# Two variances as mean squares on ScalarE, three query-key remainders on GpSimd, and new instruction orders in a one-core transformer layer

## The reference

```python
x = x + layernorm(attention(layernorm(x)))       # 16 heads of 64, T = 256
x = x + layernorm(ffn(layernorm(x)))
# attention: Q, K, V = x W + b; softmax(Q K^T / 8) V, then W_O and b_O
# ffn: gate = softmax(x @ gate_w.T) over 8 experts
#      out  = x @ weight.T + (1/16) * sum_e gate_e * lora_V[e] @ (lora_U[e] @ x)
# layernorm: (x - mean) / sqrt(var + 1e-5), no scale, no shift
```

## Time and profile before

| | us |
|---|---|
| median of three runs (1117.55 to 1120.37) | 1117.65 |
| the profiled execution, whole | 1118.4 |
| its span, first to last instruction | 1116.6 |
| busy in the span: PE | 1018.4 |
| DVE | 1022.7 |
| ACT | 833.8 |
| POOL | 678.0 |

### The profile page before, as it was taken

One profiled execution on the slowest core, in us unless ns is written; L12 is line 12 of the kernel. 1 busy time (PEld: TensorE's weight loads), 2 busy tenths in 40 slices (PEclk: granted clock), 3 DMA queues, 4 the chain that ended last, 5 costly groups with the idle time before them and its releaser, 6 DMA issues.

```text
span 1116.6 us, 28105 instructions
## 1 busy us (share of the span) xinstructions
PE 1018.4 (91%) x8550; PEld 774.4 (69%) x8550; DVE 1022.7 (92%) x2075; ACT 833.8 (75%) x2855; POOL 678.0 (61%) x682
## 2 busy tenths in 40 slices
PE   8889899999999999999999999999999999999965
PEld 7667677677677777677767667767767777767743
DVE  7899899999999999999999999999999999999962
ACT  5778777778777777877777877777877777787741
POOL 2565666565666665666665566656566666566541
PEclk9899999999999999999999999999999999999996
DMA  6555566555556655556655556655555655555660
GB/s 234 122 123 115 114 140 155 123 117 132 117 132 155 136 116 132 116 120 155 148 116 121 127 117 146 155 122 116 133 116 134 155 134 116 133 115 122 155 161 10
DMA packets 59222, 145.26 MB, mean 130 GB/s; under 512 B 17216, under 2 KB 25920, under 8 KB 59200
## 3 DMA queue, kind: packets, MB, share of 16 engines
q1 hardware_dynamic: 59200, 144.99, 56.2%
HBM read 6.50 MB, written 4.19 MB: 10 GB/s over the span
## 4 chain that ended last, share of the span: by engine, by line
POOL 42%; issue 30%; DVE 11%; PE 8%; SPq 4%; ACT 1%; POOLq 1%; DMA 1%; DVEq 0%; ACTq 0%
POOL probs L1502 32%; SPq L269 4%; POOL rstd L1482 4%; DVE neg_max L1079 4%; PE o_ps L435 3%; DVE qk_lo L1074 2%; DVE probs_b L1095 2%; POOL xn L1491 2%; POOL xn L1496 1%; POOL z L1509 1%; POOL var_eps L1475 1%; DVE stats L1003 1%; PE st_ps L413 1%; DMA probs_t<-probs_b 1%; DVE mean_var L1008 1%
## 5 line engine op out<-in xcount | busy, mean ns | idle before, releaser
L1502 POOL TENSOR_TENSOR probs<-probs,inv_sum 128x1024 f32<-128x1024 f32 x256 | 484.3, 1897 | 321.9 <-DVE inv_sum L1087 321.9
L727 ACT ACTIVATE probs<-st_ps,neg_max 128x256 f32<-128x256 f32 x1024 | 477.8, 485 | 26.3 <-DVE neg_max L1079 25.3
L1079 DVE TENSOR_REDUCE neg_max<-st_ps 128x4 f32<-128x1024 f32 x256 | 309.9, 1210 | 4.4 <-PE st_ps L413 4.0
L1095 DVE STREAM_TRANSPOSE probs_b<-probs 128x1024 f32<-128x1024 f32 x256 | 312.8, 1222 | 0.8 <-POOL probs L1502 0.8
L435 PE MATMUL o_ps<-probs_t,v_sb 128*64 128x256 f32 x2048 | 254.8, 391 | 15.6 <-DMA probs_t<-probs_b 14.7
L727 ACT ACTIVATION_READ_ACCUMULATOR probs<-st_ps,neg_max 128x1 f32 x1024 | 221.2, 216 | 0.0
L435 PEld LDWEIGHTS o_ps<-probs_t,v_sb 128*64 128x64 f32 x2048 | 138.0, 138 | 105.1 <-issue 17.8
L720 ACT CAST qk_hi<-qk_ps 128x512 fp32r<-128x512 f32 x256 | 152.5, 596 | 46.4 <-PE qk_ps L381 46.1
L413 PE MATMUL st_ps<-qk_hi 64*128 64x256 f32 x1024 | 171.7, 330 | 8.7 <-ACT probs L727 7.7
L1074 DVE TENSOR_TENSOR qk_lo<-qk_ps,qk_hi 128x512 fp32r<-128x512 f32 x256 | 170.5, 667 | 2.5 <-ACT qk_hi L720 2.2
L413 PEld LDWEIGHTS st_ps<-qk_hi 64*128 64x128 f32 x1024 | 98.0, 185 | 69.5 <-issue 44.8
(11 more groups left out here) (130 smaller groups left out, 1837.6 us busy)
## 6 DMA issues: line engine op xcount, KB each, us to landing
probs_t<-probs_b SPq DMA_DIRECT2D x1024, 128.0 KB, 2.3
out<-x_all SPq DMA_DIRECT2D x31, 128.0 KB, 2.0
x_all<-in_x SPq DMA_DIRECT2D x1, 3840.0 KB, 17.6
probs_b<-in_w_v SPq DMA_DIRECT2D x1, 512.0 KB, 4.9
probs_b<-in_w_o SPq DMA_DIRECT2D x1, 512.0 KB, 6.8
probs_b<-in_w_q SPq DMA_DIRECT2D x1, 384.0 KB, 5.4
probs_b<-in_w_k SPq DMA_DIRECT2D x1, 384.0 KB, 6.0
x_all<-in_x SPq DMA_DIRECT2D x2, 128.0 KB, 3.4
```

What stands on the lines that cost most here:

```text
L727: last = nc.scalar.activation(probs[n][:, h, j, :], st_ps[p % 2][:, (2 * h + j) * T:(2 * h + j + 1) * T], ACT.Exp, bias=neg_max[n][:, h, j ...
L1079: nc.vector.tensor_reduce(neg_max[p % N_PROBS][:, :, :].rearrange("p h j -> p (h j)"), st_ps[p % 2][:, :].rearrange("p (j s) -> p j s", j= ...
L1095: nc.vector.transpose(probs_b[chunk % 2][:, :, :, 2 * NT * n:2 * NT * (n + 1), :].rearrange("p i t n q -> p n t i q"), probs[p % N_PROBS][ ...
L1502: nc.gpsimd.tensor_tensor(probs[n][:, :, :, :].rearrange("p h j s -> p (h j) s"), probs[n][:, :, :, :].rearrange("p h j s -> p (h j) s"), ...
```

## The change

Five edits are made at once.

1. `qk_lo` of pairs 1, 4 and 6 (`POOL_LO`) moves to GpSimd, which can't read PSUM. ScalarE therefore copies the whole bank to SBUF as well (`qk_full`), besides `qk_hi`, and GpSimd subtracts from that copy. The bank is free for `project_qk` after ScalarE's two copies.
2. The layer norms of y and z take no statistics on VectorE. ScalarE squares the two tiles from PSUM and adds them up (`mean_squares`); the mean square is the variance, since the mean is zero.
3. The copies into `stats_seen` go, and statistics and aggregation of x and x1 become two steps with other work between them. At the program's end, where nothing stands between, `settle()` puts a one-column copy there.
4. The two-column gate product becomes `scale_gate_max`, two `tensor_scalar` of one column each.
5. All orders are written anew. `project_z` and `copy_z` come one sample earlier (two behind in place of three), VectorE's loop lags one sample more (its body works on pairs of samples i-3 and i-2), and `project_z` of the last samples stands elsewhere.

```diff
+POOL_LO = (1, 4, 6,)
...
-                after(pe, qk_lo_ready, PAIRS * b + p - 1)
+                if (p - 2) % PAIRS in POOL_LO:
+                    after(pe, qk_hi_ready, PAIRS * b + p - 1)
+                after(pe, *qk_bank_read(b, p - 2))
...
             def scores(b, p):
-                pe.wait_ge(qk_lo_ready, PAIRS * b + p + 1)
+                pe.wait_ge(*lo_written(b, p))
...
+            def qk_full(b, p):
+                act.wait_ge(qk_projected, PAIRS * b + p + 1)
+                sem, count = lo_written(b - 1, p)
+                after(act, sem, count)
+                nc.scalar.copy(qk_full_sb[p][:, :], qk_ps[p % 2][:, :]).then_inc(qk_full_ready, 1)
...
+            def mean_squares(ln, ps):
+                for j in range(NT):
+                    last = nc.scalar.activation(tile(squares[ln - LN_Y], j), ps[j], ACT.Square, scale=ROOT_MEAN,
+                                                accum_out=mean_square[ln - LN_Y][:, j:j + 1])
+                last.then_inc(variance_ready[ln], 1)
...
-                nc.vector.tensor_tensor(gate_neg_max[:, :], gate_max_raw[:, :], rstd[LN_X1][:, :],
-                                        ALU.mult).then_inc(gate_max_ready, 1)
+                for j in range(NT):
+                    last = nc.vector.tensor_scalar(gate_neg_max[:, j:j + 1], gate_max_raw[:, j:j + 1],
+                                                   rstd[LN_X1][:, j:j + 1], None, ALU.mult)
+                last.then_inc(gate_max_ready, 1)
...
+            def qk_lo(b, p):
+                pool.wait_ge(qk_hi_ready, PAIRS * b + p + 1)
+                pool.wait_ge(qk_full_ready, len(POOL_LO) * b + POOL_LO.index(p) + 1)
+                n = p % N_QK
+                nc.gpsimd.tensor_tensor(qk_lo_sb[n][:, :], qk_full_sb[p][:, :], qk_hi_sb[n][:, :].bitcast(F32),
+                                        ALU.subtract).then_inc(qk_pool_lo_ready, 1)
...
-                transpose_x1(i - 2, free=(v_copied[0], i + 1))
...
+                transpose_x1(i - 2, free=(x1_ready, i - 1))
...
-            project_z(29, free=(v_copied[3], 32))
-            output_projection(30, free=(z_copied, 30))
+            output_projection(30, free=(v_copied[3], 32))
```

More of the change, by code:

```diff
@@ L25 @@
 N_QK, N_PROBS = 4, 4
+POOL_LO = (1, 4, 6,)
+VECTOR_LO = tuple(p for p in range(PAIRS) if p not in POOL_LO)
 Q = 32
@@ L572, in _ @@
             scores(2, 0)
+            scores(2, 1)
             transpose_y(0, free=(yt_ready, 1))
             project_qk(2, 2)
-            scores(2, 1)
             probs_v(1, 0)
+            probs_v(1, 1)
             project_qk(2, 3)
-            probs_v(1, 1)
             project_qk(2, 4)
+            transpose_x1(0, free=(x1_ready, 1))
             scores(2, 2)
-            project_v(2, 0, free=(x1_ready, 1))
             probs_v(1, 2)
@@ new lines, in _ @@
+            run(dve, 5, B, body)
+            row_max(29, 6)
+            transpose_blocks(29, 4)
+            invert_sum(29, 5)
+            xt_low(30)
+            attention_lo(28, 3)
+            row_max(29, 7)
+            invert_sum(29, 6)
+            transpose_blocks(29, 5)
+            qk_lo(30, 0)
+            invert_sum(29, 7)
+            transpose_blocks(29, 6)
+            transpose_blocks(29, 7)
+            row_max(30, 0)
+            qk_lo(30, 2)
+            residual_x1(28)
+            row_max(30, 1)
@@ new lines, in _ @@
+            attention_lo(29, 0)
+            invert_sum(30, 0)
+            row_max(30, 2)
+            qk_lo(30, 3)
+            spread_x1(28)
+            spread_landed(LN_X1, 28)
+            settle()
+            aggregate_x1(28)
+            transpose_blocks(30, 0)
+            invert_sum(30, 1)
+            gate_max(28)
+            qk_lo(30, 5)
+            scale_gate_max(28)
+            row_max(30, 3)
+            invert_sum(30, 2)
+            apply_gate(28)
+            attention_lo(29, 1)
```

827 lines of the change are left out of this document (387 added, 440 removed).

## The result

The changed kernel takes 1090.6 us (median of four runs, 1087.9 to 1091.2) beside 1117.6 for the kernel before (four runs, 1113.7 to 1120.4): a ratio of 0.9756, 95% interval 0.9722 to 0.979. The forecast was 1087 with a range of 1067 to 1106. The profiled execution took 1091.16, its span is 1089.3.

A forecast was written before the change was run, and what follows sets the result against it. TensorE's own work plus its waits bound the period: 30.7 + 1.5 = 32.2 us against 33.16, 28 us over thirty periods. With head 0 and end 2.8, 1118.4 became 1087.6, forecast as 1087 us, range 1067 to 1106.

The forecast's parts named there:

- VectorE, ScalarE, GpSimd: Engine work per sample: VectorE falls by 4.1 to 27.5 us, ScalarE rises 3.0 to 28.9, GpSimd rises 3.9 to 25.0.
- The gate product: VectorE's gate step: two one-column products don't wait for GpSimd, saving 0.6 us; if they wait, 13 us over the run.
- TensorE's waits: Per sample after the change: 0.9 at the transposed input, 0.4 at the first projection, 0.2 at project_tg, 1.5 us together.
- the walk: One new loop body followed block by block on TensorE, asking when each input is ready; it gave waits of 1.5 us.
- TensorE's net work: TensorE's period without waits: 30.3 us before, 30.7 after, from two more changes of mode.
- The two changes of mode: TensorE's loop body goes from 20 to 22 mode changes, at 0.19 us each, 0.4 us a sample.
- The head: Before the steady part: same work in another order, taken as 0 change, within 3 us.
- The end: After the last transposed input: 2.8 us shorter, 1.5 from earlier SyncE transfers and 1.3 from z of sample 30.
- the 1.3 us at the copy of z: At the end, z of sample 30 stands ahead of the last probs_v, so the output projection saves another 1.3 us.
- Slower: Rival: ScalarE keeps over 4.3 of its 7.3 us of waits, late output projections delay scores; up to 1208 us; chance 0.09.
- ScalarE in part: Rival: ScalarE passes 0.3 to 0.8 us a period to TensorE, 1097 to 1112 us; chance 0.20, shared with gate wait.
- VectorE's 4.1 us: Per-sample VectorE saving: remainders 1.8, layer norms of y and z 1.5, two copies 0.2, gate product 0.6.

The follow-up runs named there:

- the first merge: Changed kernel with the scores of pairs 3 and 4 adjacent on TensorE, projections of pairs 6 and 7 behind them: 1084.5 us, ratio 0.9714 to before.
- gate pair product back: Changed kernel with the gate product again one two-column instruction in place of two one-column steps: 1107.2 us, ratio 0.9901 to before.
- VectorE +1.2: Changed kernel with one more 128x1024 reduction on VectorE ahead of the gate's maximum: 1089.7 us, ratio 0.9742 to before.
- ScalarE +0.6: Changed kernel with two more 256-column copies on ScalarE ahead of the gate's exponentials: 1095.9 us, ratio 0.9796 to before.
- either half alone: Changed kernel with moved work put back on VectorE, new orders kept: 1166.5 us; kernel before with all moved work, old orders kept: 1159.8 us.
- TensorE +0.96: Changed kernel with one more 256-column product for each of the eight pairs, overwritten: 1110.9 us, ratio 0.9936 to before.

## Why the prediction was right, step by step

**VectorE, ScalarE, GpSimd.** Forecast 27.5, 28.9 and 25.0 us a sample; measured 27.82, 28.48 and 24.90. The remainder on GpSimd, priced at 1.3 between ends of 0.74 and 1.9, takes 1.287. The full copy takes 0.617, and 0.48 to the next start, as priced. A square takes 0.29 with 0.22 for its accumulator, and 0.26 from the one to the next: 0.40 was forecast, between 0.36 and 0.45. So ScalarE rose by 2.62, below the bounds of 2.8 to 3.3.

**The gate product.** That it stops waiting was forecast, with 0.6 saved. The two products take 0.206 each, where 0.15 was forecast, and 0.33 together, beside a running scaling: 0.55 saved. The rule of the Trainium skill that was weighed ("VectorE: DVE Perf Modes", Mode 2×_2P, with "SBUF — State Buffer", Who interferes with whom) agrees with both rows, the new form and the old one put back. Had it failed, the forecast said 13 us; the old form put back costs 16.5.

**TensorE's waits.** Forecast 0.9 + 0.4 + 0.2 = 1.5; measured from start to start 0.93 ahead of the transposed input, 0.50 ahead of the first projection, 0.17 at y and 0.12 at tg: 1.72. The wait at y was not in the walk.

**TensorE's net work** is the term that was mis-sized: 30.7 was forecast, 32.13 - 1.72 = 30.41 measured. The two changes of mode cost 0.4 as priced, which the first merge shows. It was the 30.3 of the kernel before that held about 0.3 of gaps that are no work. One is the output projection: its 24 products took 3.06 from start to start before and take 2.88 after, and the change of mode behind it explains 0.09. Another stands just ahead of it, a wait for the copy of z too short for the profile to print: the pair projection there took 0.86 to the next start before and takes 0.71 after. That is some 0.24 of the 0.3; the rest stays open. The two errors nearly cancel, which is luck, and the period came out 0.07 short of the forecast of 32.2.

**The head** was taken as 0 within 3; it is 3.1 longer in the profiled execution. As far as the order goes, 0 was right. From the transposed input of sample 0 to that of sample 1 the kernel before takes 26.55, and a kernel with the new order of the head (scores 3 and 4 merged) takes 26.53; both have the granted clock at 1.00 nearly throughout. The changed kernel's traced execution takes 28.93 over the same order: 2.4 for the clock. The other 0.7 is a later first input (9.91, 9.19 before), and that start lies anywhere from 8.62 to 9.91 in the traces with this head. So the 3.1 is a matter of the traced execution, and no step of the walk could give it.

One thing in the new order looks as if it had a part in it, and has none that shows. GpSimd's centring of the output weights moved, from 13.99 before, onto a subtraction of VectorE with two SBUF inputs. In the timeline after:

```profile
19.98 2.61 POOL L1474 TENSOR_TENSOR probs_b<-probs_b,w_o_mean 128x1024 f32<-128x1024 f32 x1
```

```profile
21.00 2.40 DVE L986 SCALAR_TENSOR_TENSOR wk_lo<-probs_b,wk_hi 128x768 fp32r<-128x768 f32 x1
```

The two took 1.90 and 0.95 before, 6 us apart. TensorE needs `wk_lo` for the projection of pair 2 and waits 1.29 (0.62 before). With the remainders back on VectorE the two lie apart again and take 1.90 and 0.95, that wait is gone, and the head takes 28.73 all the same, at a mean clock of 0.89; more on it in the last section.

**The end** was forecast 2.8 shorter and is 0.75 shorter. That the first transfers come earlier held (28.2 after the last transposed input, 28.5 forecast, 30.5 before). It was lost behind: from the first transfers to the last output projection it takes 35.06 us, 33.40 before. In that stretch the granted clock is low: over 30 to 53 us behind the last transposed input it is 0.69, and it was 0.99.

```profile
1037.40:1060.40 23.00, 15.82 (x89) 10.04 (x86) 11.42 (x24) 9.05 (x35) 10.01 (x13) 0.69 0.82 188
1060.40:1089.30 28.90, 14.28 (x86) 9.94 (x84) 5.38 (x18) 5.82 (x23) 5.09 (x11) 0.74 0.03 10
```

How much of this is the traced execution's own is seen in three other kernels with the same order at the end: their ends took 79.12 (gate pair product back), 80.80 (VectorE +1.2) and 83.27 (ScalarE +0.6), at a clock of 0.80 to 0.85 in that stretch. The size of the end isn't settled by one trace each.

And the 1.3 us at the copy of z failed. I read TensorE's order, where z now stands ahead of the last `probs_v`, but on ScalarE `copy_z(30)` stands behind `attention_hi(31, 3)`, which waits for that very `probs_v`:

```profile
1070.73 0.39 PE L476 MATMUL extra_ps<-o_hi,wo_hi 128*128 128x256 f32 x1 [0.96 <-ACT z L793]
```

**The sum.** 1118.4 - 29.7 (998.28 - 968.61) + 3.1 - 0.75 = 1091.05; the forecast was -28 + 0 - 2.8. The steady part came out 1.7 better than forecast, head and end 5.15 worse; that is the miss of 3.5 against 1087.6. The range had allowed for head and end.

**The rivals.** "Slower" would have needed ScalarE to keep 4.3 us of waits; it keeps 3.65, just half of its 7.3. For that case the prediction has a period of 34.3, which doesn't follow from its own terms: 28.9 + 3.65 is 32.6. "ScalarE in part" is not quite empty: 0.61 us more on it costs 0.28. What no rival had is how the parts hang together: I priced VectorE's 4.1 us as a sum that need only fall below TensorE's work, and the walk gave the right waits because it used the new order and the moved work at once. With my placing, either half alone is 4% slower than before.

## What to carry to other kernels

When work moves and the order changes at once, test the four corners: here each half alone, as placed, lost 4% and the pair gained 2.4%. Price work by the stretch of the order it falls into, not by an engine's busy sum: 1.2 us more on VectorE was free in one place, 1.3 us cost 1.3 in another. Read the granted clock sample by sample before a mean period is put down to waits: 0.65 of 2.0 was the clock. Before moving a block to save a change of mode, find which engine's next step hangs on its start, and pick the place where that engine has slack.

## What the hardware showed that was not expected

The instruction order of the head is the same in the changed kernel and in the version with merged scores, yet the transposed input of sample 1 starts at 38.84 in one and at 35.43 in the other. 1.0 of this is there at the first transposed input already (9.91 and 8.90). Both have the wait for `wk_lo`, 1.29 us in one and 1.28 in the other, up to 23.50 and 22.48. Behind that wait the granted clock of the changed kernel's run stood at 0.50, the lower of the two levels (1.2 GHz); windows view:

```profile
23.50:25.00 1.50, 1.50 (x7) 1.50 (x8) 1.10 (x1) 0.18 (x1) 1.43 (x1) 0.50 0.00 0
25.00:26.50 1.50, 1.50 (x8) 1.50 (x8) 0.72 (x2) 1.34 (x5) 0.46 (x1) 0.50 0.00 0
26.50:28.00 1.50, 1.50 (x7) 0.75 (x8) 1.12 (x1) 0.93 (x4) 0.00 (x0) 0.50 0.00 0
28.00:29.50 1.50, 1.50 (x15) 1.33 (x14) 0.25 (x1) 1.23 (x5) 0.00 (x0) 0.66 0.00 0
```

In the merged version's run it stayed at full speed over the same ten microseconds:

```profile
20.00:30.00 10.00, 8.18 (x71) 6.83 (x72) 9.49 (x12) 8.23 (x28) 5.61 (x3) 1.00 0.10 36
```

Over the eight kernels with this head ("TensorE +0.96" has more products in it) the mean clock from 20 to 30 us was 0.66, 0.83 or 1.00, and the transposed input of sample 1 started between 35.4 and 38.8. In the three with the old head the clock stayed at 1.00 over these ten microseconds, and it started between 35.73 and 35.82.

The long wait there looks like the cause, and two things speak against it. In four of the eight kernels the clock fell before that wait began. In the kernel with the gate pair product back the wait begins at 22.1, and the window from 21 to 22 reads:

```profile
21.00:22.00 1.00, 1.00 (x12) 0.82 (x12) 1.00 (x1) 0.40 (x2) 1.00 (x1) 0.81 0.08 25
```

And in the kernel with the remainders back the projection of pair 2 starts at 22.11 without any wait, and the clock is low all the same; windows view of that run:

```profile
22.00:25.00 3.00, 3.00 (x17) 2.90 (x14) 1.86 (x3) 1.93 (x5) 1.89 (x1) 0.52 0.01 3
```

What lowers it in the head stays open. In the steady part the picture is clearer. The clock stayed at 1.00 in twelve of the fourteen kernels; their longest printed waits in a sample are 0.75 to 1.27 us. In the two that wait 1.50 to 1.56 for the input's remainder it fell during that wait or just behind it, in 3 of 7 samples of one and in 2 of 9 of the other, and each such sample took 0.3 to 2.5 us longer. The same wait in the samples between left it at 1.00, so the wait goes with the fall and isn't enough for it.

The 2.4 us are seen between traces of kernels with the same order in the head; no kernel was traced twice. Scores 3 and 4 merged and gate pair product back ran on one chip and took 26.53 and 28.81 from sample 0 to sample 1, so the chip isn't what parts them. Kernels closer than some 3 us are told apart here by their periods only.
